# A staged second load of x, its group statistics a span earlier, and more key tiles summed on VectorE

## The reference, cut to what matters

```python
x = x + attention(_gn(x), W_qkv, W_proj, b_proj)   # layer 0
x = x + displace(_gn(x), offset)                   # layer 1

def _gn(v, G=32, eps=1e-5):        # mean and variance over each of 32 groups
    g = v.reshape(B_, G, C_ // G, H_, W_)
    return ((g - mean(g)) / sqrt(var(g) + eps)).reshape(v.shape)

# attention, 12 heads of 64 channels, N = 1024 positions
var_v, var_k = var(v, -1, ddof=1), var(k, -1, ddof=1)
out = softmax(var_v @ var_k.T * scale) @ v         # scores of rank one
out = out @ W_proj.T + b_proj
# displace: each channel shifted by whole pixels, then a 3x3 depthwise kernel
```

## Time and profile before

| | |
|---|---|
| median of 3 runs | 2066.14 us (2064.36 to 2068.34) |
| the profiled execution | 2068.55 us, span 2066.8 us |
| TensorE busy | 2002.8 us, 97% |
| VectorE busy | 1668.6 us, 81% |
| ScalarE busy | 1207.0 us, 58% |
| POOL busy | 264.3 us, 13% |
| chain that ended last | TensorE 58%, VectorE 20%, DMA 8% |

### The profile page before, as it was taken

One profiled execution on the slowest core, in us unless ns is written; L12 is line 12 of the kernel. 1 busy time (PEld: TensorE's weight loads), 2 busy tenths in 40 slices (PEclk: granted clock), 3 DMA queues, 4 the chain that ended last, 5 costly groups with the idle time before them and its releaser, 6 DMA issues.

```text
span 2066.8 us, 33759 instructions
## 1 busy us (share of the span) xinstructions
PE 2002.8 (97%) x12924; PEld 1115.2 (54%) x12924; DVE 1668.6 (81%) x3594; ACT 1207.0 (58%) x1321; POOL 264.3 (13%) x323
## 2 busy tenths in 40 slices
PE   3999999999999999999999999999999999999997
PEld 3756347662565536554376634766256553655443
DVE  6688576997679976898769987699867997699857
ACT  3576734776267743778527783477626774377820
POOL 2100001111012100111001210111101210011121
PEclk9999999999999999999999999999999999999998
DMA  8212303445044541446114561344603454144514
GB/s 324 83 53 63 103 1 102 133 130 180 2 124 144 162 116 42 126 129 205 45 63 126 158 178 22 99 130 133 184 2 124 144 162 116 42 128 132 147 35 183
DMA packets 104978, 236.33 MB, mean 114 GB/s; under 512 B 46704, under 2 KB 47472, under 8 KB 104816
## 3 DMA queue, kind: packets, MB, share of 16 engines
q0 software_dynamic: 31968, 116.41, 19.4%
q1 hardware_dynamic: 66800, 95.74, 15.3%
q10 hardware_dynamic: 6048, 22.02, 3.1%
HBM read 154.06 MB, written 79.73 MB: 113 GB/s over the span
## 4 chain that ended last, share of the span: by engine, by line
PE 58%; DVE 20%; DMA 8%; issue 7%; ACT 5%; SPq 1%; ACTq 0%; POOL 0%; DVEq 0%; POOLq 0%
PE ps L1303 23%; PE ps L1360 16%; PE ps L1345 14%; DVE bt L885 7%; ACT ring L671 5%; DVE st L837 3%; DMA a_sb<-a_rows 3%; PE ps L1320 2%; DMA dt_sb<-d_sb 2%; DMA a_rows<-at 1%; DVE bst_x L811 1%; DMA bt<-r_rows 1%; DVE bt L1008 1%; DVE bt L1005 1%; SPq L447 1%
## 5 line engine op out<-in xcount | busy, mean ns | idle before, releaser
L671 ACT ACTIVATE ring<-a_sb,coef 128x1024 f32<-128x1024 f32 x768 | 817.7, 1137 | 23.5 <-issue 12.3
L1303 PE MATMUL ps<-wkv_hi,h_sp 128*128 128x256 f16 x4608 | 771.8, 273 | 3.9 <-DVE h_sp L828 2.4
L1345 PE MATMUL ps<-ring,xv 128*64 128x512 f32 x3072 | 691.3, 597 | 6.2 <-ACT ring L671 5.1
L1303 PE MATMUL ps<-wkv_lo,h_sp 128*128 128x256 f16 x2304 | 628.8, 273 | 0.0
L885 DVE TENSOR_TENSOR bt<-bt,ring 128x1024 f32<-128x1024 f32 x464 | 541.8, 1212 | 3.0 <-ACT ring L671 1.7
L1303 PEld LDWEIGHTS ps<-wkv_hi,h_sp 128*128 128x128 f16 x4608 | 451.5, 98 | 85.5 <-issue 28.5
L1345 PEld LDWEIGHTS ps<-ring,xv 128*64 128x64 f32 x3072 | 207.7, 137 | 427.0 <-issue 385.1
L655 ACT ACTIVATE xv<-ps 128x256 f32<-128x256 f32 x192 | 72.7, 383 | 511.8 <-DVE st L837 510.9
L1360 PE MATMUL ps<-xv,wp_hi 128*128 128x512 f16 x1152 | 349.7, 380 | 0.0
L837 DVE BATCH_NORM_STATS2 st<-ps 128x6 f32<-128x64 f32 x1536 | 217.0, 211 | 123.4 <-PE ps L1303 122.6
L1303 PEld LDWEIGHTS ps<-wkv_lo,h_sp 128*128 128x128 f16 x2304 | 225.7, 98 | 26.6
(11 more groups left out here) (164 smaller groups left out, 1397.9 us busy)
## 6 DMA issues: line engine op xcount, KB each, us to landing
a_sb<-a_rows SPq DMA_DIRECT2D x96, 512.0 KB, 5.4
out<-xv POOLq DMA_DIRECT2D x84, 512.0 KB, 5.3
xv<-in_x POOLq DMA_DIRECT2D x48, 512.0 KB, 3.7
h_sp<-in_x ACTq DMA_DIRECT2D x42, 512.0 KB, 5.3
shift_rows<-bt POOLq DMA_DIRECT2D x42, 512.0 KB, 3.4
bt<-r_rows SPq DMA_DIRECT2D x80, 256.0 KB, 4.0
shift_rows<-ring SPq DMA_DIRECT2D x12, 528.0 KB, 15.3
xv<-in_L_conv_W_qkv SPq DMA_DIRECT2D x4, 1152.0 KB, 14.2
```

What stands on the lines that cost most here:

```text
L671: nc.scalar.activation(ring_of(p, s, m), a_sb[:, h % 4, :], ACT.Exp, scale=coef[:, h, m:m + 1]).then_inc(s_exp, 1)
L1303: last = nc.tensor.matmul(ps[:, kv_bank[u % 2], half * 2 * P:(half + 1) * 2 * P], h_sp[:, k, hp, m * P:(m + 1) * P], wkv[wpart][:, k, q * ...
L1345: last = nc.tensor.matmul(ps[s * HD:(s + 1) * HD, o_bank[p % 2] + j, :], v_sb[:, p, m, s * HD:(s + 1) * HD], ring_of(p, s, m)[:, j * HALF: ...
```

## The change

- `MD` becomes (7, 8, 8, 8, 6, 7).
- SP loads the x of batch b + 2 a second time. `stage_x` stands at the head of SP's body, before `y_chain`, and waits until batch b's exponentials, sums and denominators and layer 1 of the batch before are done. Its six tiles go to `x_st`: two buffers of `ring`, `t_t` and the three of `acc`.
- VectorE takes the statistics of these tiles beside units 0 to 2, 4 and 5 of phase_a and the first unit of the span. `channel_aggregate` moves to pair 4, tile 3, `group_var` to pair 4, tile 7, `group_spread_x` to pair 5, tile 4; the SP and POOL steps between move with them.
- `x_in` is loaded as before; `make_h` now waits for it tile by tile.
- `h_second` stands behind projection units 0 to 5 instead of 6 to 11.
- In pair 5 VectorE's sums of tiles 4 to 6 are issued together at tile 4, ahead of `o_normalise`; `d_reciprocal_last` and `o_second` of pair 4 follow there, ahead of `taps_x` of channel tile 5.
- For the step from batch 0 to batch 1 the statistics of x are still taken in `group_end`, all six tiles behind `d_reciprocal_last`.

```diff
+        x_st = [ring[:, 6, :], ring[:, 7, :], t_t] + [acc[:, i, :] for i in range(3)]
-        MD = (7, 8, 8, 8, 5, 5)
+        MD = (7, 8, 8, 8, 6, 7)
@@ SP: span, stage_x, body
+                    if p == 4 and later and with_next:
+                        stats_to_groups(sp, "x", b)
                 if with_next:
-                    stats_to_groups(sp, "x", b)
+                    if not later:
+                        stats_to_groups(sp, "x", b)
...
+            def stage_x(b):
+
+                sp.wait_ge(s_pv, b * (NT // 2))
+                sp.wait_ge(s_acc, b * NADD)
+                hold(sp, s_held_sp)
+                if b > 1:
+                    sp.wait_ge(s_fin, (b - 1) * CT)
+                    hold(sp, s_held_sp)
+                sp.wait_ge(s_d, b * NP)
+                for t in range(CT):
+                    sp.dma_start(x_st[t], x_t[b + 1, :, t, :]).then_inc(s_xst[t], 16)
+
             def body(b, with_next):
+                if with_next:
+                    stage_x(b + 1)
                 y_chain(b)
@@ POOL: layer1, at the end of turn t
+                    if t == CT - 1 and with_next:
+                        group_pow(pool, "x", b + 1)
@@ ScalarE: make_h, then span
+                        act.wait_ge(s_xin[t], b * 16 + 16)
...
+                        if later and with_next and p == 0 and m == 3:
+                            act.wait_ge(s_bst["x"], (b + 1) * PU + 6)
@@ VectorE: staged_stats, phase_a
+            def staged_stats(b, t):
+                dve.wait_ge(s_xst[t], (b - 1) * 16)
+                for j in (0, 1):
+                    nc.vector.bn_stats(bst["x"][:, t, j, :], x_st[t][:, j * HALF:(j + 1) * HALF]).then_inc(s_bst["x"], 1)
...
+                    if staged and u <= 2:
+                        staged_stats(b + 1, u)
...
+                    if staged and u >= UQ:
+                        staged_stats(b + 1, u - 1)
@@ VectorE: span
                     if p == 0:
                         kv_stats(b, nxt)
+                        if staged:
+                            staged_stats(b + 1, CT - 1)
...
-                        if m < MT - 1:
+                        if m < (MT - 1 if p < NP - 1 else 4):
                             add_up(b, p, m, later)
+                        if (p, m) == (NP - 1, 4):
+                            for n in range(4, MT - 1):
+                                add_up(b, p, n, later)
...
                             if p == 4:
                                 a_out(b, p + 1, later)
+                                if staged:
+                                    channel_aggregate("x", b + 1)
...
                             if p:
                                 o_normalise(b, p - 1)
+                            if p == NP - 1:
+                                if staged:
+                                    group_spread_x(dve, b, H_UP)
+                                d_reciprocal_last(b)
+                                o_second(b, p - 1)
...
-                        if m == 7 and p:
+                        if m == 7 and 1 <= p <= 4:
                             o_second(b, p - 1)
-                            if p == NP - 1 and with_next:
-                                x_stats(b + 1, range(3))
+                            if p == 4 and staged:
+                                group_var(dve, "x", b)
@@ VectorE: group_end
-                if with_next:
-                    x_stats(b + 1, (3,))
-                d_reciprocal_last(b)
-                if with_next:
-                    x_stats(b + 1, (4,))
+                first_next = with_next and b == 0
+                if first_next:
+                    x_stats(b + 1, range(4))
                 o_normalise_last(b)
...
-                    if with_next and u >= PU - CT:
+                    if first_next and u >= PU - CT:
                         h_second(b + 1, u - (PU - CT))
+                    if with_next and not first_next and u < CT:
+                        h_second(b + 1, u)
```

More of the change, by code:

```diff
@@ L220, in gn_attention_displace @@
         s_xin = [sem(f"s_xin{t}") for t in range(CT)]
+        s_xst = [sem(f"s_xst{t}") for t in range(CT)]
         s_bst = {k: sem(f"s_bst_{k}") for k in "xy"}
@@ L542, in k_reduce, with layer1 @@
                 nc.gpsimd.partition_all_reduce(kall[:, :], kmx[:, :], P, ABSMAX).then_inc(s_kall, 1)
-            def layer1(b):
+            def layer1(b, with_next):
                 for t in range(CT + 1):
@@ L600, in body @@
                 group_pow(pool, "y", b)
-                layer1(b)
-                if with_next:
-                    group_pow(pool, "x", b + 1)
+                layer1(b, with_next)
             def last(b):
@@ L1022, in taps_x, with phase_a @@
                                                ALU.mult, ALU.add).then_inc(s_fin, 1)
-            def phase_a(b, l1, beside=None):
+            def phase_a(b, l1, with_next, beside=None):
+                staged = l1 is not None and with_next
                 for u in range(UA):
@@ L1041, in phase_a @@
                         k_scales(b, 0)
+                    if staged and u >= UQ:
+                        staged_stats(b + 1, u - 1)
             def span(b, l1, with_next, beside=None):
                 later = l1 is not None
+                staged = later and with_next
                 for p in range(NP):
@@ L1091, in group_end @@
             def group_end(b, with_next, in_halves=False):
-                if with_next:
-                    x_stats(b + 1, (3,))
-                d_reciprocal_last(b)
-                if with_next:
-                    x_stats(b + 1, (4,))
+                first_next = with_next and b == 0
+                if first_next:
+                    x_stats(b + 1, range(4))
                 o_normalise_last(b)
-                if with_next:
-                    x_stats(b + 1, (5,))
+                if first_next:
+                    x_stats(b + 1, (4, 5))
                     channel_aggregate("x", b + 1)
                 o_second(b, NP - 1)
-                if with_next:
+                if first_next:
                     group_var(dve, "x", b)
@@ L1255, in beside_span @@
                             stage()
-                phase_a(0, None, beside_a)
+                phase_a(0, None, True, beside_a)
                 span(0, None, True, beside_span)
@@ L1262, in body @@
                 group_end(b, True)
-                phase_a(b + 1, b)
+                phase_a(b + 1, b, with_next)
                 span(b + 1, b, with_next)
```

## The result

The changed kernel takes 2114.31 us (median of 4 runs, 2113.49 to 2116.78) against 2066.81 us of the kernel before, timed beside it on the same chip: the ratio is 1.0215, with a 95% interval of 1.0195 to 1.0235. It is slower, by 47.5 us where 31.6 were forecast: above the forecast's own range (2086 to 2110), and just inside the one given for 8 in 10 (2056 to 2116). The profiled execution took 2114.7 us, with a span of 2113.0 (2066.8 before).

The account below looks back on a forecast made before the run. TensorE was taken as the bound (busy 242.37 of 244.72 us a batch). Five transitions +37.8, the last +0.4, reciprocal waits and clock dip -5.2, ends +0.8 - 2.2: together +31.6 us, so 2098, range 2086 to 2110.

Parts of the forecast that it names:

- Direction, place and chain: Slower: late last taps delay POOL's store, the reload, ScalarE's h, its split and an eviction, stalling TensorE in the projection.
- The first rival: Loads and reload don't slow each other, group statistics land early: stall 0.2 us, 2047; chance 0.17 together with a 2062 variant.
- T: Moment at which the last pair's denominators are complete; forecast to move by +0.5 us, bounds -1.9 and +3.
- Step 0 to 1: Batch 0 to 1: x statistics behind the reciprocal delay o_normalise and first eviction; +0.8 us after 3.0 gained in batch 0.
- The clock: Projection, behind each stall: 1.7 us lost to a lower clock, as after an earlier wait of 1.40 us.
- rival 4: The reload lands behind all six loads and the clock is back later: +54 us, 2120; chance 0.10.
- the second row of the table: T to the first key/value matmul, summed over seven transitions: forecast +35.8 us.
- The group sums of x: Pair 4, VectorE: DRAM round trip lands at 1470.5, delaying pair 5's sums by 5.8 us; T at +0.5 instead of -1.9.
- the first row: Last variances of pair 4 to T, summed over eight batches: forecast -2.2 us.
- Sums on VectorE fit: Pair 5: VectorE's added sums, 7.1 us, fit where four x tiles of statistics, 4.84 us, leave; T moves -1.9 at best.
- rival 3: The edit of the sums does nothing, since ScalarE paces pair 5; stall about what is saved: 2066 us; chance 0.08.
- rival 2: The stall comes, but the group statistics land early and the sums pay: +17 us, 2083; chance 0.20.

Follow-up runs that it names:

- the two kernels with all three edits: Changed kernel with group sums awaited in pair 5, loads behind the reload, taps ahead of the reciprocal: 2057.57 us; the same with MD set back: 2068.57 us.

## Why the prediction was right, and where its sizes were off

- **Direction, place and chain** held, and were shown by taking links away: the loads behind the reload, or the taps ahead of them, each bring the kernel down by some 35 to 39 us. The signs named for it are all there: POOL's store of 9.39 us or more, ScalarE's idle time ended by the bias add, VectorE's ahead of the group sums. The first rival, on the other side, fell on its first half, a store of 9.91 us beside the loads and 5.11 without them.
- **Size of the stall**: 5.7 us forecast, 4.97 to 5.82 measured, in the five transitions named and not in the sixth (0.2 forecast, 0.34 measured). The step that sized it, the excess of a store beside half the loads taken for store and reload together, was good here: 5.3 us taken, and the bias add began 4.6 to 5.5 us later after T in these five than in 6 to 7. That it is no more beside six loads than beside two or three was taken without a row, so that it came so close is in part luck.
- **Step 0 to 1**: forecast +3.8 before the gain of batch 0, measured +4.3: 1.43 us of wait for o_normalise and 2.50 at the first eviction, against 1.7 and 2.0.
- **The clock** was the first mis-sized term: "I add as much" (1.7 us for each stall) took a wait of 1.40 us as the measure of one of 5. Behind the five stalls 13.4 us went, 2.7 each; less the old dip of 1.7 that is 11.7, where 5 x 1.7 - 1.7 = 6.8 were forecast. With 1.5 us less of waits than forecast (30.9 for 5 x 5.7 + 0.2 + 3.7 = 32.4), 3.4 of the 4.2 us by which the second row of the table exceeds the forecast are accounted for. Of rival 4 the clock's later return was right, its still later reload not; the measured time lies nearer to its 2120 than to 2098, but more than half of the way there was made by the next term.
- **The group sums of x** were the second: "so I take 1470.5". That is 12.1 us after the issue at 1458.4. Its own sum, 1464.3 and some 5 more, would give 1469.3. In batch 5 VectorE had them 15.36 us after the issue, beyond the bound of 1473 (14.6); in the other five batches 13.15 to 14.43, and the issue itself came on average 0.5 us later behind the variances than forecast. Mean over the six staged batches, T moved by +2.27 us, where +0.5 was forecast: 6 x 1.77 = 10.6. That is the 10.2 us of the first row, with 0.4 gained at the ends. What was off is the choice of the row: I priced two transfers of 6 KB by a quiet stretch and added the excess of one slow store, where each of the two is slow (6.9 to 8.7 us for the write, against 4.0; 5.7 to 6.7 for the read, against 1.6). The direct trial (group sums awaited in pair 5) gives 24.7 us for this term, where the forecast had 6 x 2.4 = 14.4. The wait hits TensorE twice: as waits for exponentials, 31.2 us against 5.1, and by the clock behind these, 3.8 us in L1390.
- **Sums on VectorE fit**, as forecast, but only with the x statistics gone from there: alone they made the kernel slower by 49.9 us (2116.13 against 2066.28 on that chip). With the group sums out of the way they bring T forward by 2.2 to 3.6 us in batches 1 to 6 (the two kernels with all three edits, with these sums and without), more than the "-1.9 at best". So rival 3 fell, and rival 2 with the landing of the group sums.
- **The rest of the batch** gained 2.5 us for 2.0 forecast: the split of h, 2.4 us of waits before, is down to 0.3, and the staged statistics beside the first key/value units cost nothing there.
- **No luck in the sum**: the rows of the table miss by +10.2, +4.2 and -0.5 us, so the two mis-sized terms add up and don't cancel.

## What to carry to other kernels

Follow a moved instruction through the queues behind it, on other engines too: here two taps on VectorE set a POOL store, that a reload, that ScalarE's h, and only that TensorE. Loads into idle buffers weren't free here: released within a microsecond of a transfer on the path, they held it up by 4.4 to 4.9 us (9.39 to 9.91 against 5.01); ordering them behind it cost nothing that shows. A round trip through DRAM, awaited in an in-order engine, belongs where the engine arrives after its worst landing, not its usual one.

## What the runs showed of the hardware

Transfers of 6 KB took far longer in a busy stretch (DMA share 0.89 from 1494.48 to 1509.84 of the changed kernel) than in a quiet one (0.07 in the 5.9 us of the kernel before). The listing of DMA issues (line, count, KB each, median us from issue to landing) shows the same two transfers for x, moved, and for y, left where they were, in the changed kernel:
```profile
cs_rows_x<-mv_x SPq DMA_DIRECT2D x7, 6.0 KB, 7.1
gin_x<-cs_rows_x SPq DMA_DIRECT2D x7, 6.0 KB, 6.0
...
cs_rows_y<-mv_y SPq DMA_DIRECT2D x7, 6.0 KB, 4.0
gin_y<-cs_rows_y SPq DMA_DIRECT2D x7, 6.0 KB, 1.7
```
13.1 us for the pair against 5.7. Where x stood before, its two medians were 4.0 and 1.6. It doesn't take the x loads to slow the write: with all of them in pair 5 (the kernel with the later x loads) they overlap only its last 0.2 to 4.4 us, and it took 8.2 to 9.8. The a_sb rows just ahead of it on the same queue and POOL's transfers are left, and no run separates them.

Two waits for exponentials of nearly one length, 2.10 and 2.38 us in pair 5 of batch 5, were followed by different clocks. Windows of the changed kernel from each on, over the same 16 matmuls of L1390:
```profile
1514.79:1518.80 4.01, 3.87 (x17) 1.03 (x18) 4.01 (x5) 2.03 (x2) 0.00 (x0) 1.00 0.43 149
...
1523.88:1529.16 5.28, 5.28 (x20) 1.49 (x24) 5.21 (x9) 2.64 (x3) 0.00 (x0) 0.69 0.15 55
```
4.01 us at a granted clock of 1.00, and 5.28 at 0.69. Ahead of the second the 4.01 us of work lay between two waits, the first of 2.10. But that doesn't settle it: a wait of 2.37 or 2.38 us stands at this place in each of batches 1 to 6, and only in 4 and 5 was the clock lower over the next 5.28 us (0.68 and 0.69, against 1.00 in the other four); in batch 4 the wait before it was 0.23 us, in batch 6, without a dip, 0.84. What decides is not shown here. The mean granted clock of the run fell from 0.994 to 0.979.
